# A packed product over 48 contraction rows, made a product over all 128 rows with zero weights below

## The chip, the cores and the metric

The kernel runs on one core of a Trainium2 chip. The metric is the device time in microseconds (us) of one execution; for one core that is the time of that core. A core has the engines TensorE (PE in the profile, its weight loads listed apart as PEld), VectorE (DVE), ScalarE (ACT), GpSimd (POOL) and SyncE (SP), which run their own instruction streams and wait for each other through semaphores, and 16 DMA engines that move data between HBM and the on-chip memory SBUF.

## What is computed

Cut to what matters, the reference is this:

```python
# x: (10000, 128), adj: (10000, 10000), float32
h = item_feat @ W_item.T + b_item              # (10000, 128)
b = layernorm(x) @ W_user.T + b_user
x = x + relu(adj @ h + b)                      # the big product
# then a mixture of 8 experts, top 1, with a capacity of 1563 rows each
n = layernorm(x); probs = softmax(n @ gate_w + gate_b); idx = argmax(probs)
x = x + y_of_expert[idx](n) * prob             # relu(n @ w1 + b1) @ w2 + b2
```

Nearly all of the arithmetic and all of the 400 MB that are read are `adj @ h`.

## The kernel before

**The big product.** The 10000 users (rows of `adj`) are taken in 20 blocks of 500. The host has transposed `adj`, so that a block is a stack of chunks of 128 items by 500 users: 78 full chunks (`FULL`) and a remainder of 16 items (`REM`). For each chunk TensorE holds 128 items x 128 features of `h` as weights and streams 500 users past them; the sums stay in one PSUM bank (`acc[q]`, two banks that blocks use in turn). Chunks are loaded in groups of 4, 20 groups a block (`GROUPS`), the last one of 2 full chunks and the remainder.

**Three products for one.** Matmuls run on operands of the reduced type fp32r, and the precision of fp32 is made up by splitting both sides into a high and a low part: `h_hi*a_hi` and `h_lo*a_hi` (`high_part`, L949 and L951) and `h_hi*a_lo` (`low_part`, L960). ScalarE makes `a_hi` from the loaded `raw` (`high`, L440), into a ring of 4 groups; VectorE subtracts and makes `a_lo` in place of `raw` (`low`, L604), a ring of 10 groups.

**The remainder.** The 16 items of the remainder are handled in one matmul, in place of three: `PACK` is 48, and the rows 0 to 47 of the last chunk of `h_hi` hold `h_hi`, `h_lo` and `h_hi` again, 16 rows each, against `a_hi`, `a_hi` and `a_lo` in the same rows of a slot of the ring. The rows 16 to 47 of the weights are put there once by two small DMAs (`pack_h`, issued on SP's queue in block 1). This is L967, once a block, 20 times in all. It ends the accumulation of its block (`stop=True`), and its end raises `lo_used`.

**Order on TensorE.** It is written out by hand, in `body`: `high_part` of group g, then `low_part` of group g-1, and small products for other stages after chosen groups. So the last `low_part` of a block, with L967 as its last matmul, stands behind `high_part` of group 0 of the next block and ahead of `high_part` of group 1. Behind the last block it stands by itself, ahead of the small products of that block's routing.

**Who waits for L967.** ScalarE waits for `lo_used` of the whole block before it casts group 3 of the next block (the ring slot of group 3 is the one that L967 reads), and before it takes the sums out of the bank (`take_gnn`, L449). SP waits for `lo_used` group by group before it reloads `raw`.

**Around it.** The blocks' routing (layernorm, gate, slots) runs on VectorE and GpSimd one and two blocks late, between the large instructions. GpSimd scatters each block's rows by indirect DMA (`scatter`, L849 and L853), 8 of them a block; in the last block it also clears unused slots (L860, L867, L875). After the 20 blocks comes the expert stage: 32 units of 392 rows, whose records are loaded by SP, with L1067 to L1098 on TensorE.

**Start.** VectorE fills some constants and raises `set_up` with each; TensorE waits for four of these (`pe.wait_ge(set_up, 4)`), for the constants and for the first items before its first product `h_chunks` (L932).

Of the kernel before, what the change touches and what calls it, by code (L numbers as in the profile page):

```python
# [5 lines left out]
ALU = mybir.AluOpType  # L6
# [6 lines left out]
HID = 128  # L13
# [6 lines left out]
BLOCK = TILES * TP  # L20
BLOCKS = USERS // BLOCK
FULL = ITEMS // 128
REM = ITEMS - FULL * 128
PACK = 3 * REM
CHUNKS = FULL + 1
# [5 lines left out]
HI_RING = 4  # L31
# [43 lines left out]
def build(nc, adj_m, adj_r, items_t, x, consts, item_consts, w1, w2, rec_d, out):  # L75
    ctx = ExitStack()
    with ctx:
        def sb(name, shape, dt=F32):
            return ctx.enter_context(nc.sbuf_tensor(name, shape, dt))

        def sem(name):
            return ctx.enter_context(nc.semaphore(name))
# [4 lines left out]
        def const(name, rows=128):  # L87
            a, b = COLS[name]
            return cst[0:rows, a:b]

        ident = const("ident")
        h_hi = sb("h_hi", [128, CHUNKS * HID], F32R)
# [6 lines left out]
        a_hi = sb("a_hi", [128, HI_RING, GMAX * BLOCK], F32R)  # L99
# [84 lines left out]
        acc = bank[0:2]  # L184
# [17 lines left out]
        set_up = sem("set_up")  # L202
# [75 lines left out]
        def blocks(eng, body):  # L278

            for i in range(PEEL // 2):  # L280
                for q in range(2):
                    body(i, q)
            with eng.Fori(PEEL // 2, BLOCKS // 2 - 1) as i:
                for q in range(2):
                    body(i, q)
            for q in range(2):
                body(BLOCKS // 2 - 1, q)
# [42 lines left out]
        @block.sync  # L330
        def _(sp):
            def load_items(g):
                if g >= 2:
                    sp.wait_ge(h_product, g - 1)
                a = FIRST[g] * 128
                b = min(a + SIZES[g] * 128, ITEMS)
                sp.dma_start(items[:, g % 2, 0:b - a], items_t[:, a:b]).then_inc(items_loaded[g % 2], 16)

            def body(i, q):
                b = i * 2 + q  # L340
                fixed = isinstance(b, int)
                for g in range(GROUPS):
                    if not fixed or b > 0 or g >= RAW:
                        sp.wait_ge(lo_used, b * GROUPS + g - RAW + 1)
                    last = g == GROUPS - 1
                    n = (SIZES[g] - last) * BLOCK
                    a = FIRST[g] * BLOCK
                    adj_b = adj_m[b] if fixed else adj_m[bass.ds(b, 1), :, :].rearrange("o p n -> (o p) n")
                    sp.dma_start(raw[:, g % RAW, 0:n], adj_b[:, a:a + n],
                                 max_dma_last_dim=16384).then_inc(raw_loaded[g % RAW], 16)  # L350
                    if fixed and b == 1 and g == 2:
                        pack_h()
                    if last:
                        rem_b = adj_r[b] if fixed else adj_r[bass.ds(b, 1), :, :].rearrange("o p n -> (o p) n")
                        sp.dma_start(raw[0:PACK, g % RAW, n:n + BLOCK], rem_b).then_inc(raw_loaded[g % RAW], 16)
                    if fixed and b == 0 and g + 2 < GROUPS:
                        load_items(g + 2)

            def pack_h():

                sp.wait_ge(h_lo_ready, GROUPS)
                cols = slice(FULL * HID, CHUNKS * HID)
                sp.dma_start(h_hi[REM:2 * REM, cols].bitcast(F32), h_lo[0:REM, cols].bitcast(F32)).then_inc(h_packed, 16)
                sp.dma_start(h_hi[2 * REM:PACK, cols].bitcast(F32), h_hi[0:REM, cols].bitcast(F32)).then_inc(h_packed, 16)

            sp.dma_start(cst[:, :], consts).then_inc(consts_loaded, 16)
            sp.dma_start(gnn[:, 0:2 * HID], item_consts).then_inc(consts_loaded, 16)
            load_items(0)
            load_items(1)
            blocks(sp, body)  # L370


            def load_weights(e, slot_, wait):
                if wait:
                    sp.wait_ge(yT_ready, (e - 1) * UNITS_E)
                w1_e = w1[bass.ds(e, 1), :, :].rearrange("o p n -> (o p) n")
                w2_e = w2[bass.ds(e, 1), :, :].rearrange("o p n -> (o p) n")
                sp.dma_start(wb1[:, slot_, :], w1_e).then_inc(weights_loaded[slot_], 16)
                sp.dma_start(wb2[:, slot_, :], w2_e).then_inc(weights_loaded[slot_], 16)

            rec_units = rec_d.rearrange("(r j) c -> r (j c)", j=4)

            def load_rec(q, k, wait):
                if wait:
                    sp.wait_ge(toki_ready, q - BODY + 1)
                    sp.wait_ge(yout_ready, q - BODY + 1)
                sp.dma_start(recq[:, k, :, :].rearrange("p j c -> p (j c)"),
                             rec_units[bass.ds(q * SLOT_P, SLOT_P), :]).then_inc(recq_loaded[k], 16)

            sp.wait_ge(edges_cleared, 16)  # L390
            sp.wait_ge(runs_cleared, EXPERTS * 16)
            sp.wait_ge(lo_used, BLOCKS * GROUPS)
            load_weights(0, 0, False)
            for q in range(2):
                sp.wait_ge(scattered[q], BLOCKS // 2 * TILES * 16)
            for k in range(BODY):
                if k == 2:
                    load_weights(1, 1, False)
                load_rec(k, k, False)
            with sp.Fori(1, UNITS // BODY) as i:  # L400
                for k in range(BODY):
                    if k % UNITS_E == 2:
                        load_weights(i * 2 + k // UNITS_E, k // UNITS_E, True)
                    load_rec(i * BODY + k, k, True)
            for q in range(2):
                sp.wait_ge(passed_on[q], BLOCKS // 2 * TILES * 16)
            for k in range(2):
                sp.wait_ge(sent[k], UNITS // 2 * 64)
# [157 lines left out]
        def _(dve):  # L566
            v = nc.vector
# [10 lines left out]
            def h_bias(g):  # L578
                dve.wait_ge(h_product, g + 1)
                n, a = SIZES[g], FIRST[g] * HID  # L580
                m = n - 1 if g == GROUPS - 1 else n
                last = v.tensor_tensor(h_raw[:, a:a + m * HID].rearrange("p (c d) -> p c d", d=HID),
                                       ps_h[g % 2][:, 0:m * HID].rearrange("p (c d) -> p c d", d=HID),
                                       b_item.unsqueeze(1).broadcast_to([128, m, HID]), ALU.add)
                if m < n:
                    last = v.tensor_tensor(h_raw[0:REM, a + m * HID:a + n * HID], ps_h[g % 2][0:REM, m * HID:n * HID],
                                           b_item[0:REM, :], ALU.add)
                last.then_inc(h_biased, 1)
# [178 lines left out]
            v.memset(neghalf[:, :], -0.5).then_inc(set_up, 1)  # L767
            dve.wait_ge(consts_loaded, 32)
            v.tensor_copy(tok[:, :, :].rearrange("p a j -> p (a j)"), const("tok", TP)).then_inc(set_up, 1)
            dve.wait_ge(set_up, 4)  # L770
            h_bias(0)
            h_low(0)
            h_bias(1)
# [56 lines left out]
        def _(pool):  # L830
# [60 lines left out]
                if not fixed or b < BLOCKS - 1:  # L891
                    x_scale(b + 1)

            pool.wait_ge(set_up, 4)
            x_scale(0)
            blocks(pool, body)
            x1_scale(BLOCKS - 1, 1)
# [26 lines left out]
        def _(pe):  # L924
# [30 lines left out]
            def low_part(b, q, g):  # L955

                pe.wait_ge(lo_ready, b * GROUPS + g + 1)
                for c in range(min(SIZES[g], FULL - FIRST[g])):
                    k = FIRST[g] + c
                    last = nc.tensor.matmul(acc[q][:, 0:BLOCK], h_hi[:, k * HID:(k + 1) * HID],  # L960
                                            a_lo[:, g % RAW, c * BLOCK:(c + 1) * BLOCK],
                                            start=False, stop=False)
                if g == GROUPS - 1:
                    if isinstance(b, int) and b == 0:
                        pe.wait_ge(h_packed, 32)
                    c = FULL - FIRST[g]
                    last = nc.tensor.matmul(acc[q][:, 0:BLOCK], h_hi[0:PACK, FULL * HID:CHUNKS * HID],  # L967
                                            a_hi[0:PACK, g % HI_RING, c * BLOCK:(c + 1) * BLOCK],
                                            start=False, stop=True)
                last.then_inc(lo_used, 1)  # L970

# [74 lines left out]
                        logits(b - 1)  # L1046

            pe.wait_ge(consts_loaded, 32)
            pe.wait_ge(set_up, 4)
            h_chunks(0)  # L1050
            h_chunks(1)
            blocks(pe, body)
            low_part(BLOCKS - 1, 1, GROUPS - 1)
            count(BLOCKS - 2)
            turn_gnn(BLOCKS - 1)
# [109 lines left out]
```

## Time and profile before

| | |
|---|---|
| runs of the kernel before | 1458.34 us median of 3 (1447.47, 1458.34, 1459.8) |
| the profiled execution | 1444.59 us, its span 1442.6 us |
| mean granted TensorE clock | 0.971 |
| TensorE busy | 1356.5 us, 94% of the span |
| VectorE, ScalarE, GpSimd busy | 1169.6, 981.6, 569.6 us |
| HBM read, written | 422.79 MB, 23.50 MB |
| L967, the packed product | 20 times, 9.9 us busy in all |

Busy is the union of the instructions' spans. Matmuls overlap, so the sum of their durations is longer than the time they take: how fast TensorE goes is read from where one matmul starts and where the next one does. The profiled execution was quicker than each of the three timed runs.

### The profile page before, as it was taken

The numbers are of one execution on the slowest core, as the hardware profiler recorded it, in microseconds if no ns is written. First come the engines' busy times: TensorE is split into PE (matmuls) and PEld (weight loads), VectorE is DVE, ScalarE is ACT, GpSimd is POOL, SyncE is SP. The second block draws the span as 40 slices with busy tenths as digits, with TensorE's granted clock in tenths as the row PEclk, the third lists the DMA queues.
The fourth block names the chain that finished last, engine by engine and source line by source line (L and its number), as shares of the span: only waits on it lengthen the run. The fifth ranks groups of instructions, "written<-read, shape, count | busy, mean of one in ns | idle before, by whom it ended". The sixth has DMA issues, their size and how long they took to land. (4 is left out here: it accounts for less than half of the span.)

```text
span 1442.6 us, 20384 instructions
## 1 busy us (share of the span) xinstructions
PE 1356.5 (94%) x6278; PEld 1109.0 (77%) x6278; DVE 1169.6 (81%) x1714; ACT 981.6 (68%) x1010; POOL 569.6 (39%) x426
## 2 busy tenths in 40 slices
PE   7999999999999999999999999999999952998893
PEld 6888888888888888888888888888888842776662
DVE  7898988989889889888898898898988931677665
ACT  5677876777768767767677687677776713877661
POOL 0001235144053251350541523514405365576777
PEclk9999999999999999999999999999999975999997
DMA  8999999999999999999999999999999723122220
GB/s 326 358 393 407 399 381 348 371 357 357 365 356 358 372 354 354 374 352 362 361 365 356 362 359 358 360 358 367 360 359 369 285 87 91 51 85 73 66 59 3
DMA packets 89072, 435.59 MB, mean 302 GB/s; under 512 B 22558, under 2 KB 24774, under 8 KB 89032
## 3 DMA queue, kind: packets, MB, share of 16 engines
q1 hardware_dynamic: 68000, 417.72, 78.4%
q0 software_dynamic: 17952, 12.25, 3.2%
q10 hardware_dynamic: 3080, 5.12, 1.1%
q8 instruction: 21, 0.34, 0.1%
q14 instruction: 19, 0.16, 0.0%
HBM read 422.79 MB, written 23.50 MB: 309 GB/s over the span
## 5 line engine op out<-in xcount | busy, mean ns | idle before, releaser
L604 DVE TENSOR_TENSOR a_lo<-raw,a_hi 128x2000 fp32r<-128x2000 f32 (+1 forms) x400 | 862.2, 2188 | 127.6 <-ACT a_hi L440 124.1
L440 ACT CAST a_hi<-raw 128x2000 fp32r<-128x2000 f32 (+1 forms) x400 | 721.4, 1826 | 180.8 <-PE bank L951 111.6
L949 PE MATMUL bank<-a_hi,h_hi 128*128 128x500 f32 x1560 | 626.2, 401 | 0.9 <-ACT a_hi L440 0.8
L951 PE MATMUL bank<-a_hi,h_lo 128*128 128x500 f32 x1560 | 606.9, 389 | 0.0
L960 PE MATMUL bank<-a_lo,h_hi 128*128 128x500 f32 x1560 | 417.9, 388 | 0.0
L949 PEld LDWEIGHTS bank<-a_hi,h_hi 128*128 128x128 f32 x1560 | 293.6, 188 | 65.9 <-issue 10.6
L951 PEld LDWEIGHTS bank<-a_hi,h_lo 128*128 128x128 f32 x1560 | 294.5, 189 | 59.1 <-issue 4.4
L960 PEld LDWEIGHTS bank<-a_lo,h_hi 128*128 128x128 f32 x1560 | 293.3, 188 | 59.3
L841 POOL TENSOR_TENSOR late<-ve,neghalf 125x4 f32<-125x4 f32 x20 | 57.2, 2861 | 649.6 <-DVE ve L621 649.6
L849 POOL DMA_INDIRECT records<-late,slot x80 | 182.3, 2278 | 22.9 <-issue 22.6
L915 POOL DMA_INDIRECT out<-raw,toki x128 | 136.5, 1066 | 37.1 <-issue 36.8
L853 POOL DMA_INDIRECT out<-late,kept_out x80 | 116.3, 1454 | 24.4 <-issue 24.4
L1098 PE MATMUL bank<-raw 128*128 128x392 f32 x256 | 92.5, 504 | 5.8 <-issue 5.8
L553 ACT ACTIVATE raw<-bank,raw 128x392 f32<-128x392 f32 x128 | 66.5, 587 | 21.4 <-remote 16.0
L481 ACT COPY colsT<-bank 128x500 f32<-128x500 f32 x20 | 11.5, 577 | 99.3 <-PE bank L1000 83.7
L1098 PEld LDWEIGHTS bank<-raw 128*128 128x128 f32 x256 | 49.3, 195 | 35.3 <-issue 9.3
L544 ACT ACTIVATE raw<-raw 98x128 f32<-98x128 f32 x128 | 53.1, 494 | 19.5 <-DMA raw<-records 19.5
L837 POOL TENSOR_TENSOR xrs<-xve,neghalf 125x4 f32<-125x4 f32 x20 | 26.5, 1327 | 89.5 <-DVE xve L621 89.1
L798 DVE TENSOR_TENSOR a_hi<-bank,a_hi 128x392 fp32r<-128x392 f32 x32 | 18.1, 564 | 51.8 <-ACT a_hi L538 41.2
L1087 PE MATMUL bank<-a_hi 128*128 128x392 f32 x128 | 48.5, 379 | 5.2 <-issue 2.9
L325 POOL TENSOR_TENSOR carrier_pool<-ones 125x1 f32<-125x1 f32 x52 | 34.0, 655 | 44.4 <-issue 36.1
L1089 PE MATMUL bank<-a_hi 128*128 128x392 f32 x128 | 45.5, 355 | 0.0
(116 smaller groups left out, 938.0 us busy)
## 6 DMA issues: line engine op xcount, KB each, us to landing
raw<-adj_m SPq DMA_DIRECT2D x380, 1000.0 KB, 6.7
raw<-adj_m SPq DMA_DIRECT2D x20, 500.0 KB
raw<-records SPq DMA_DIRECT2D x32, 202.1 KB
late<-items_t SPq DMA_DIRECT2D x19, 256.0 KB, 4.8
xb<-x ACTq DMA_DIRECT2D x20, 224.0 KB
raw<-w SPq DMA_DIRECT2D x8, 258.5 KB
raw<-w SPq DMA_DIRECT2D x8, 256.0 KB
out<-raw,toki POOLq DMA_INDIRECT x128
```

Of the source, the lines that this page charges most:

```text
L440: last = nc.scalar.copy(a_hi[:, g % HI_RING, 0:m], raw[:, g % RAW, 0:m])
L544: last = nc.scalar.activation(x2q[:, k % 2, j, :], recq[:, k, j, 0:HID], ACT.Identity, scale=recq[:, k, j, C_RSTD:C_RSTD + 1], bias=recq[: ...
L553: nc.scalar.activation(hm[:, (k - LAG_MID) % 2, f, :], ps_mid[f][:, 0:UNIT], ACT.Relu, bias=bias_of(k, LAG_MID, f)).then_inc(hm_ready, 1)
L604: last = v.tensor_tensor(a_lo[:, g % RAW, 0:m], raw[:, g % RAW, 0:m], a_hi[:, g % HI_RING, 0:m].bitcast(F32), ALU.subtract)
L841: p.tensor_tensor(rec[:, q, :, C_RSTD:C_RSTD + 1], ve[:, :].unsqueeze(2), neghalf[:, :].unsqueeze(2), ALU.pow).then_inc(rstd_ready, 1)
L849: p.indirect_dma_start(rec_d, bass.IndirectOffsetOnAxis(ap=slot[:, q, j:j + 1], axis=0), rec[:, q, j, :], None, bounds_check=SLOTS - 1, oo ...
L853: p.indirect_dma_start(out, bass.IndirectOffsetOnAxis(ap=kept_out[:, q, j:j + 1], axis=0), rec[:, q, j, 0:HID], None, bounds_check=USERS - ...
L915: p.indirect_dma_start(out, bass.IndirectOffsetOnAxis(ap=toki[:, (k - LAG_OUT) % BODY, j:j + 1], axis=0), yout[:, (k - LAG_OUT) % 2, j, :] ...
L949: nc.tensor.matmul(acc[q][:, 0:BLOCK], h_hi[:, k * HID:(k + 1) * HID], a, start=(k == 0), stop=False)
L951: last = nc.tensor.matmul(acc[q][:, 0:BLOCK], h_lo[:, k * HID:(k + 1) * HID], a, start=False, stop=False)
L960: last = nc.tensor.matmul(acc[q][:, 0:BLOCK], h_hi[:, k * HID:(k + 1) * HID], a_lo[:, g % RAW, c * BLOCK:(c + 1) * BLOCK], start=False, st ...
L1098: last = nc.tensor.matmul(ps_y[:, 0:UNIT], wb2[:, w, f * HID:(f + 1) * HID], hm[:, (k - LAG_Y) % 2, f, :], start=(f == 0), stop=(f == FC - 1))
```

## The change

L967 reads all 128 rows of the last chunk of `h_hi` and of the ring slot, in place of rows 0 to 47. So that rows 48 to 127 add nothing, VectorE writes zeros into rows 32 to 127 of the last chunk of `h_hi` at the start (two `tensor_scalar`, `ident` times 0.0, of 32 and of 64 rows by 128 columns), and `pack_h` fills rows 32 to 47 with `h_hi` later, now after a wait for the zeros. The ring slot's rows 48 to 127 hold there what an earlier group's cast left; it is multiplied by zero. `set_up` now counts to 6, and VectorE, GpSimd and TensorE wait for 6 in place of 4.

```diff
             def pack_h():
+                sp.wait_ge(set_up, 6)
                 sp.wait_ge(h_lo_ready, GROUPS)
...
             v.tensor_copy(tok[:, :, :].rearrange("p a j -> p (a j)"), const("tok", TP)).then_inc(set_up, 1)
-            dve.wait_ge(set_up, 4)
+            for lo, hi in ((32, 64), (64, 128)):
+                v.tensor_scalar(h_hi[lo:hi, FULL * HID:CHUNKS * HID], ident[lo:hi, :], 0.0, None,
+                                ALU.mult).then_inc(set_up, 1)
+            dve.wait_ge(set_up, 6)
             h_bias(0)
...
-            pool.wait_ge(set_up, 4)
+            pool.wait_ge(set_up, 6)
             x_scale(0)
...
-                    last = nc.tensor.matmul(acc[q][:, 0:BLOCK], h_hi[0:PACK, FULL * HID:CHUNKS * HID],
-                                            a_hi[0:PACK, g % HI_RING, c * BLOCK:(c + 1) * BLOCK],
+                    last = nc.tensor.matmul(acc[q][:, 0:BLOCK], h_hi[:, FULL * HID:CHUNKS * HID],
+                                            a_hi[:, g % HI_RING, c * BLOCK:(c + 1) * BLOCK],
                                             start=False, stop=True)
...
-            pe.wait_ge(set_up, 4)
+            pe.wait_ge(set_up, 6)
             h_chunks(0)
```

No instruction changes places on TensorE, ScalarE, GpSimd or SP. On VectorE two rows are added at its start. Before:

```order
L767 MEMSET neghalf 125x4
L769 COPY tok<-cst 125x8
L582 TENSOR_TENSOR h_raw_49<-bank5,gnn 128x512
L594 TENSOR_TENSOR h_lo<-h_raw_49,h_hi 128x512
L582 TENSOR_TENSOR h_raw_49<-bank6,gnn 128x512
```

And in the changed kernel:

```order
L768 MEMSET neghalf 125x4
L770 COPY tok<-cst 125x8
L772 TENSOR_SCALAR h_hi<-cst 32x128
L772 TENSOR_SCALAR h_hi<-cst 64x128
L583 TENSOR_TENSOR h_raw_49<-bank5,gnn 128x512
L595 TENSOR_TENSOR h_lo<-h_raw_49,h_hi 128x512
L583 TENSOR_TENSOR h_raw_49<-bank6,gnn 128x512
```

The two zero writes stand between the last of the old constants and the first bias of `h`, and TensorE's first product waits for them.

## Rows read from the trace of the kernel before

**Rows 1.** The page: granted TensorE clock in 40 slices of the span.

```profile
PEclk9999999999999999999999999999999975999997
```

**Rows 2.** Busy time by stage: blocks 2 to 18, and all that follows block 19's big product.

```profile
core 0: us, PE busy (x) PEld busy (x) DVE busy (x) ACT busy (x) POOL busy (x), PEclk, DMA share, GB/s
143.00:1112.00 969.00, 969.00 (x4432) 797.58 (x4431) 842.76 (x1155) 695.07 (x561) 350.06 (x187) 1.00 0.99 363
1170.30:1442.60 272.30, 194.49 (x921) 150.64 (x920) 156.35 (x355) 152.05 (x336) 180.75 (x220) 0.85 0.24 67
```

**Rows 3.** Line L967 from 143 to 1112 us: its matmuls (ns), and who waited.

```profile
L967 PE MATMUL bank<-a_hi,h_hi x17: 494/494/494, 143.4 to 1057.0; 48*128 48x500 f32 x17
...
  ACT a_hi L440: 39.0, 17
```

**Rows 4.** Timeline of PE, 598 to 603 us: start, us, engine, line, instruction.

```profile
599.45 0.39 PE L951 MATMUL bank<-a_hi,h_lo 128*128 128x500 f32 x1
599.68 0.61 PE L960 MATMUL bank<-a_lo,h_hi 128*128 128x500 f32 x2
600.22 0.49 PE L967 MATMUL bank<-a_hi,h_hi 48*128 48x500 f32 x1
600.64 0.49 PE L949 MATMUL bank<-a_hi,h_hi 128*128 128x500 f32 x1
600.98 0.39 PE L951 MATMUL bank<-a_hi,h_lo 128*128 128x500 f32 x1
...
602.57 0.62 PE L960 MATMUL bank<-a_lo,h_hi 128*128 128x500 f32 x2
```

**Rows 5.** Timeline of the weight loads there; in brackets the idle time ahead.

```profile
600.22 0.18 PEld L967 LDWEIGHTS bank<-a_hi,h_hi 48*128 48x128 f32 x1 [0.34 <-issue]
600.64 0.19 PEld L949 LDWEIGHTS bank<-a_hi,h_hi 128*128 128x128 f32 x1 [0.24 <-issue]
```

**Rows 6.** Timeline of PE, 610 to 612.5 us: the matmul behind L1013 and L1014.

```profile
611.98 0.47 PE L949 MATMUL bank<-a_hi,h_hi 128*128 128x500 f32 x1
```

**Rows 7.** Waits from 143 to 1112 us: total, times, longest.

```profile
DVE a_lo L604 <- ACT a_hi L440: 114.3, 51, 5.8
ACT a_hi L440 <- PE bank L951: 105.5, 128, 1.7
```

**Rows 8.** Timelines of the start, and of VectorE at 82 us.

```profile
5.67 0.17 DVE L769 COPY tok<-cst 125x8 f32<-125x8 f32 x1 [4.64 <-DMA gnn<-item_consts]
6.29 3.49 PEld L932 LDWEIGHTS bank<-gnn,late 128*128 128x128 f32 x16 [6.29 <-DMA gnn<-item_consts]
...
82.20 0.27 DVE L596 TENSOR_TENSOR h_lo<-h_raw,h_hi 16x128 fp32r<-16x128 f32 x1
```

**Rows 9.** Timelines of ScalarE, VectorE and GpSimd in the last block and behind it.

```profile
1114.73 3.63 ACT L440 CAST a_hi<-raw 128x2000 fp32r<-128x2000 f32 x2 [2.33 <-PE bank L967]
...
1116.62 2.24 DVE L604 TENSOR_TENSOR a_lo<-raw,a_hi 128x2000 fp32r<-128x2000 f32 x1 [0.48 <-ACT a_hi L440]
...
1149.52 8.69 DVE L604 TENSOR_TENSOR a_lo<-raw,a_hi 128x2000 fp32r<-128x2000 f32 x4
...
1175.21 0.17 DVE L621 TENSOR_SCALAR ve<-mv 125x4 f32<-125x4 f32 x1
...
1141.09 2.94 POOL L841 TENSOR_TENSOR late<-ve,neghalf 125x4 f32<-125x4 f32 x1 [33.22 <-DVE ve L621]
...
1149.79 9.48 POOL L849 DMA_INDIRECT records<-late,slot  x1 [0.30 <-DVE clear_edge L701]
...
1161.48 1.19 POOL L849 DMA_INDIRECT records<-late,slot  x1 [0.30 <-issue]
...
1182.08 1.05 POOL L841 TENSOR_TENSOR late<-ve,neghalf 125x4 f32<-125x4 f32 x1
```

**Rows 10.** The chain that ended last, in the expert stage.

```profile
1303.84 4.50 PE bank L1098 x8
...
1316.84 2.64 PE bank L1098 x8
```

## The prediction

> **What bounds the kernel now.** I read the stages first. [...] A busy TensorE is not yet a TensorE at its pace, so next I look at the pace. L967 starts 17 times between 143.4 and 1057.0 us [rows 3]: 913.6 us over 16 blocks is 57.10 us a block. [...]
>
> [...]
>
> **What one packed product costs.** I read distances from start to start. Between L951 at 600.98 and the L960 pair at 602.57 lie seven ordinary distances, 1.59 us, so 0.227 us for one matmul of 500 columns [rows 4]. From the L960 pair at 599.68 over L967 at 600.22 and L949 at 600.64 to L951 at 600.98 lie four distances: at the ordinary pace 0.91 us, in the trace 1.30. So a packed product costs 0.39 us more than an ordinary one in its place. The parts: the second L960 starts one ordinary distance behind 599.68, at 599.91, so L967 follows it by 0.31 (0.08 too much); L949 follows L967 by 0.42 (0.19 too much); L951 follows L949 by 0.34 (0.11 too much). The weight loads show the shape of it. Ordinarily a weight load runs beside the matmul ahead of it; here the load of L967 starts together with its matmul, after 0.34 us in which the load path did nothing ("issue": no event that the profile knows), and the next load, of L949, again starts with its matmul after 0.24 us [rows 5]. The stall stands on both sides of the one instruction whose rows are 48. L967 itself lasts 0.494 us in place of some 0.39, the same in all 17 [rows 3, 4].
>
> What is different about L967? Its type, its 500 columns and its 128 weight columns are those of its neighbours. Its sum closes a bank and the next matmul writes the other bank, but each block boundary changes banks between groups, and the step from L951 of the new block to L960 of the old one (599.45 to 599.68) is ordinary [rows 4]. It raises a semaphore, but so does the last L960 of every group. What is left is the number of rows, 48 against 128. By that reading, the change makes it an ordinary matmul.
>
> [...]
>
> **The change, part by part.**
> - *The stall goes*, 0.39 us for each packed product with ordinary matmuls on both sides. Twenty products; for the last one only L967's late start and its longer duration could count, 0.08 + 0.11 = 0.19.
> - *The path to the end* takes fewer than all of them. In the last block the cast of group 3 begins when L967 of block 18 is done (ScalarE had waited 2.33 us for it), VectorE's L604 at 1116.62 waited for that cast, and from there VectorE runs without a pause up to the variance that releases GpSimd's L841 at 1141.09 [rows 9]. GpSimd then works without a pause through scatters and clears until 1182.08, where it takes up a variance that VectorE had finished at 1175.38. So the end hangs on GpSimd, which hangs on the end of L967 of block 18. What TensorE wins after that (0.30 behind this L967, 0.19 at the last) runs into GpSimd's lead of 1182.08 - 1175.38 = 6.70 us and is worth nothing. On the path lie 18 whole stalls, of blocks 0 to 17, and 0.19 of block 18: 18 x 0.39 + 0.19 = 7.2 us. If all of TensorE's gain counted it would be 19 x 0.39 + 0.19 = 7.6.
> - *What is late next in a block*: the cast of group 3 waits for L967's end. ScalarE waits 39.0 us in 17 times for it, 2.3 each, and then needs 1.8 us. TensorE wants group 3 four parts behind L967, after `high_part` 1, `low_part` 0, `high_part` 2 and `low_part` 1: 24 matmuls of 0.227, or 5.4 us. The slack is 3.5 us against the 0.30 that L967's end comes closer, so this stays covered. The loads move 363 GB/s and must go 0.7% faster; the waits show no lateness there [rows 7].
> - *Two zero writes at the start.* The trace has no such instruction. The nearest rows are the copy ahead of it, 0.17 us, and a subtraction of 128 columns, 0.27 [rows 8]. The copy ends at 5.84, so the zeros are done between 6.18 and 6.38; TensorE's first weight load began at 6.29, put down to a DMA. The cost is 0 to 0.1 us, and it would go on to all that follows since the first products release the item loads. Nothing can get earlier by it. I take 0.05.
> - *The other waits*: SP's new wait in `pack_h` stands ahead of a wait for the last part of `h_lo`, made at 82.20 us [rows 8], long after the zeros; the reloads of `raw` queued behind are not held up by it. GpSimd's first work needs a variance that VectorE makes behind the first two biases of `h`, after the zeros in any case. Both cost nothing.
> - *More rows read*: weight load 0.18 against 0.19 for the neighbours [rows 5], so at most 0.01 a block, and beside other work.
>
> Sum: 7.2 - 0.05 = about 7.1 us. The profiled execution took 1444.59 us (2.0 of it outside the span of 1442.6), which gives 1437.5. That execution was the quickest of the four known; the median of the timed runs is 1458.34, and against that the same saving gives **1451.2 us**, a ratio of 0.995. The spread of the runs before, 1447.47 to 1459.8, is larger than the effect. Within 1% is about what a measurement of this kernel can tell from no change.
>
> **Rivals.**
> 1. *The stall has another cause and stays.* For it: the 0.47 us duration of an L949 behind the small products of 125 rows [rows 6] is much like the 0.49 behind L967, so a long L949 alone needs no 48 rows (the small products have another type, which L967 has not). Against it: the idle load path ahead of L967 itself. Time: 1458.3, or 1444.6 for the profiled one. [...] Chance 0.10.
> 2. *A scatter of the last block falls under VectorE.* The scatter at 1149.79 took 9.48 us against 1.19 at 1161.48; VectorE ran four L604 in a row beside it, 8.69 us from 1149.52 [rows 9]. That is a price of 8.3 us on the path that sets the end. GpSimd and VectorE hang on the same L967, so their distance should stay; if it moves by the few tenths that let one more scatter begin inside such a run, 8.3 is lost and 7.1 won: **1.2 us slower than before**, 1459.5. It decides from the point at which a scatter that now ends in time begins inside such a run. The same mechanism the other way would free up to the 6.70 us of lead, and give 1444.5. [...] Chance 0.04 slower, 0.04 faster.
> 3. *The expert stage meets more of the low clock.* [...] Chance 0.04 for four or more.
>
> **How the numbers follow.** The forecast has 0.78, and the four cases above 0.22. Its own range runs from 1437.0 (the quickest execution less 7.6) to 1452.7 (the slowest less 7.1). To hold the time 8 times in 10 I take 1435 to 1456, a stretch of low clock less at one end and two more at the other; most of rival 1 is left out. Faster by over 1% needs 14.6 us: the freed scatter, or runs of the two kernels that fall at different ends of a spread of 12.3; 0.12. Slower by over 1% needs the reverse without the gain: 0.03. Within 1%: 0.85.
>
> **What the profile of the changed kernel would show.** L967's successor with 128 rows, some 0.39 us long, its weight load beside the matmul ahead of it and with no idle time of 0.34; the next L949 0.227 behind it. L967's successor starts every 56.7 us in place of 57.10. TensorE still fully busy from 143 us on. ScalarE still waits at group 3, about as long as now. First weight load at 6.3 to 6.4. The last packed product near 1162.4, GpSimd's second L841 near 1175. Wrong would be: a distance that stays at 0.42 behind it; a block that is shorter while the span is not, which would put the loss into GpSimd's scatters or the expert stage.

## The result, and the profile of the changed kernel

| | before | changed |
|---|---|---|
| median of 22 runs | 1455.03 us (1441.31 to 1464.82) | 1446.91 us (1435.42 to 1454.16) |
| ratio of the times | | 0.9955, 95% interval 0.9936 to 0.9974 |
| profiled execution, its span | 1444.59, 1442.6 us | 1449.17, 1447.2 us |

The change makes the kernel 0.45% faster by the ratio, 6.5 us of 1455 (the two medians lie 8.1 us apart). The two profiled executions alone would say the opposite, by 4.6 us, so the profile must be read stage by stage. First the timeline of TensorE at the packed product (now L971) of the changed kernel:

```profile
596.55 0.61 PE L964 MATMUL bank<-a_lo,h_hi 128*128 128x500 f32 x2
597.00 0.39 PE L971 MATMUL bank<-a_hi,h_hi 128*128 128x500 f32 x1
597.23 0.39 PE L953 MATMUL bank<-a_hi,h_hi 128*128 128x500 f32 x1
597.45 0.39 PE L955 MATMUL bank<-a_hi,h_lo 128*128 128x500 f32 x1
```

and of its weight loads:

```profile
596.32 0.42 PEld L964 LDWEIGHTS bank<-a_lo,h_hi 128*128 128x128 f32 x2
596.78 0.19 PEld L971 LDWEIGHTS bank<-a_hi,h_hi 128*128 128x128 f32 x1
597.00 0.19 PEld L953 LDWEIGHTS bank<-a_hi,h_hi 128*128 128x128 f32 x1
```

The four distances that took 1.30 us in [rows 4] take 0.90 here. The load of L971 starts 0.22 us ahead of its matmul, beside the matmul before it, and neither load has an idle time in brackets, where [rows 5] have 0.34 and 0.24. The line's own view, from 138 to 1104 us, and the busy times of the stages:

```profile
L971 PE MATMUL bank<-a_hi,h_hi x17: 392/392/392, 143.3 to 1050.7; 128*128 128x500 f32 x17
...
  ACT a_hi L441: 35.8, 17
```

```profile
core 0: us, PE busy (x) PEld busy (x) DVE busy (x) ACT busy (x) POOL busy (x), PEclk, DMA share, GB/s
143.00:1105.00 962.00, 962.00 (x4430) 798.64 (x4428) 842.21 (x1155) 693.99 (x561) 346.70 (x187) 1.00 0.99 365
1162.80:1447.20 284.40, 200.12 (x922) 150.16 (x920) 156.47 (x355) 153.22 (x336) 177.60 (x221) 0.85 0.23 64
```

907.4 us over 16 blocks is 56.71 us a block, against 57.10 in [rows 3]: 0.39 less, with TensorE still busy all the time. The stage behind the big product took 284.40 us against 272.30 in [rows 2], 12.1 longer; that is the whole of the contradiction. The change has no instruction there. On the quicker chips of the experiments the stage is as long with the stall as without it: from the start of the last packed product to the end of the span it took 257.9 us with 48 rows (all of the change but the matmul, below) and 257.6 in the changed kernel, one trace each.

The timeline of GpSimd in the last block and behind it, and that of the start, VectorE and TensorE:

```profile
1134.28 2.93 POOL L845 TENSOR_TENSOR late<-ve,neghalf 125x4 f32<-125x4 f32 x1 [33.02 <-DVE ve L622]
...
1142.96 9.49 POOL L853 DMA_INDIRECT records<-late,slot  x1 [0.30 <-DVE clear_edge L702]
...
1175.08 1.06 POOL L845 TENSOR_TENSOR late<-ve,neghalf 125x4 f32<-125x4 f32 x1
1182.73 0.20 POOL L325 TENSOR_TENSOR carrier_pool<-ones 125x1 f32<-125x1 f32 x1 [6.60 <-issue]
```

```profile
5.37 0.17 DVE L770 COPY tok<-cst 125x8 f32<-125x8 f32 x1 [4.34 <-DMA gnn<-item_consts]
5.57 0.47 DVE L772 TENSOR_SCALAR h_hi<-cst 32x128 fp32r<-32x128 f32 x2
...
6.14 3.58 PE L936 MATMUL bank<-gnn,late 128*128 128x128 f32 x16 [6.14 <-DVE h_hi L772]
```

GpSimd's second L845 starts at 1175.08 in place of 1182.08 [rows 9], 7.0 us earlier, with the same long scatter ahead of it (9.49 against 9.48). The zeros end at 6.04 and TensorE's first product starts at 6.14, released by them. In the kernel before a load of items released it:

```profile
6.32 0.98 PE L932 MATMUL bank<-gnn,late 128*128 128x128 f32 x3 [6.32 <-DMA late<-items_t]
```

From the start of VectorE's copy of the constants to the first product it is 0.65 us there (5.67 in [rows 8] to 6.32), and 0.77 in the changed kernel.

### The profile page after: what moved, and what is told of

The parts are those of the page before. It is cut to its first block and busy times, and to the rows that moved or that the text cites. A ratio compares the mean times of both kernels' runs of the same rounds, so it can differ in the third digit from the quotient of the medians.

```text
span 1447.2 us, 20387 instructions
## 1 busy us (share of the span) xinstructions
PE 1354.0 (94%) x6278; PEld 1110.0 (77%) x6278; DVE 1169.5 (81%) x1716; ACT 981.9 (68%) x1010; POOL 562.4 (39%) x426
## 3 DMA queue, kind: packets, MB, share of 16 engines
q1 hardware_dynamic: 68000, 417.72, 77.8%
## 5 line engine op out<-in xcount | busy, mean ns | idle before, releaser
L845 POOL TENSOR_TENSOR late<-ve,neghalf 125x4 f32<-125x4 f32 x20 | 57.2, 2859 | 645.8 <-DVE ve L622 645.8
L853 POOL DMA_INDIRECT records<-late,slot x80 | 178.7, 2233 | 22.9 <-issue 22.6
L919 POOL DMA_INDIRECT out<-raw,toki x128 | 132.6, 1036 | 38.6 <-issue 38.3
L1102 PE MATMUL bank<-raw 128*128 128x392 f32 x256 | 96.9, 523 | 9.2 <-issue 6.9
```

The source lines that it names most:

```text
L845: p.tensor_tensor(rec[:, q, :, C_RSTD:C_RSTD + 1], ve[:, :].unsqueeze(2), neghalf[:, :].unsqueeze(2), ALU.pow).then_inc(rstd_ready, 1)
L853: p.indirect_dma_start(rec_d, bass.IndirectOffsetOnAxis(ap=slot[:, q, j:j + 1], axis=0), rec[:, q, j, :], None, bounds_check=SLOTS - 1, oo ...
L919: p.indirect_dma_start(out, bass.IndirectOffsetOnAxis(ap=toki[:, (k - LAG_OUT) % BODY, j:j + 1], axis=0), yout[:, (k - LAG_OUT) % 2, j, :] ...
L1102: last = nc.tensor.matmul(ps_y[:, 0:UNIT], wb2[:, w, f * HID:(f + 1) * HID], hm[:, (k - LAG_Y) % 2, f, :], start=(f == 0), stop=(f == FC - 1))
```

## The experiments

They ran on three chips, each beside runs of the kernel before: 64 rows, 96 rows, all but the matmul and two in a row beside a single one of 1429.06 us; 32 rows, the padding, the early clears and the changed kernel again beside a median of 1429.37 (9 runs); the two with pauses beside a median of 1429.04 (7 runs). Only the changed kernel again, the early clears, and the clears with the pauses were timed more than once; the others are single executions, and are read by their traces. All these runs of the kernel before are quicker than every one of the 22 above, and lie closer together.

### How many rows stall: 64, 96, 32

```diff
-                    last = nc.tensor.matmul(acc[q][:, 0:BLOCK], h_hi[:, FULL * HID:CHUNKS * HID],
-                                            a_hi[:, g % HI_RING, c * BLOCK:(c + 1) * BLOCK],
+                    last = nc.tensor.matmul(acc[q][:, 0:BLOCK], h_hi[0:64, FULL * HID:CHUNKS * HID],
+                                            a_hi[0:64, g % HI_RING, c * BLOCK:(c + 1) * BLOCK],
                                             start=False, stop=True)
```

(and 0:96, 0:32 in the same places of the changed kernel).

> The changed kernel with the packed product over rows 0 to 63 in place of all 128. If a matmul over at most 64 rows among full ones is what stalls TensorE, the stall is whole again: the product starts 0.31 us behind its predecessor and its successor 0.42 behind it, 57.10 us a block. If the stall hung on the odd count of 48 or on a partly filled group of 32 rows (48 is one and a half), 64 rows are free of it: 0.227 on both sides, 56.71 us a block.

> The changed kernel with the packed product over rows 0 to 95. If only products of at most 64 rows change how the array is divided, this one is ordinary: 0.227 us on both sides, 56.71 us a block. If any row count other than that of the neighbours stalls, 0.31 and 0.42 are back and a block takes 57.10 us.

> The changed kernel with the packed product over rows 0 to 31 (the low part of the adjacency's remainder is left out). If a change of the division costs the same whichever it is, 0.31 and 0.42 us, 57.10 us a block, as with 48 and 64 rows. If the stall follows the number of rows, it differs from that of 48.

The view of line L971 from 143 to 1080 us in the kernel with 64 rows:

```profile
L971 PE MATMUL bank<-a_hi,h_hi x17: 494/494/494, 142.9 to 1056.5; 64*128 64x500 f32 x17
```

with 96 rows:

```profile
L971 PE MATMUL bank<-a_hi,h_hi x16: 391/391/392, 199.1 to 1049.7; 96*128 96x500 f32 x16
```

with 32 rows:

```profile
L971 PE MATMUL bank<-a_hi,h_hi x17: 492/492/493, 143.0 to 1056.5; 32*128 32x500 f32 x17
```

64 rows: 913.6 over 16 is 57.10 us a block, the stall is whole, 1427.51 us in all. 32 rows: 913.5 over 16 is 57.09, 1431.6 us. 96 rows: 850.6 over 15 (the first product of the other views falls just ahead of 143 us here) is 56.71, no stall, 1420.4 us. So it is no matter of rows that fill a group of 32, nor of being equal to the neighbours: 32, 48 and 64 rows cost the same, 96 and 128 cost nothing. The limit lies above 64 and not above 96; no run had a number in between. What TensorE does inside at the change is not shown: the "division" that the expectations here and below speak of was my reading, and no run places products of 32 and of 64 rows next to each other. The weight loads of the kernel with 64 rows show the picture of [rows 5] again:

```profile
599.72 0.18 PEld L971 LDWEIGHTS bank<-a_hi,h_hi 64*128 64x128 f32 x1 [0.34 <-issue]
600.14 0.19 PEld L953 LDWEIGHTS bank<-a_hi,h_hi 128*128 128x128 f32 x1 [0.24 <-issue]
```

### All of the change but the matmul

```diff
-                    last = nc.tensor.matmul(acc[q][:, 0:BLOCK], h_hi[:, FULL * HID:CHUNKS * HID],
-                                            a_hi[:, g % HI_RING, c * BLOCK:(c + 1) * BLOCK],
+                    last = nc.tensor.matmul(acc[q][:, 0:BLOCK], h_hi[0:48, FULL * HID:CHUNKS * HID],
+                                            a_hi[0:48, g % HI_RING, c * BLOCK:(c + 1) * BLOCK],
                                             start=False, stop=True)
```

> The changed kernel with everything of the change but the matmul itself: the zero writes and the waits for six stay, the product reads rows 0 to 47. By my theory the whole gain is in the rows of the matmul: 57.10 us a block as before, stall 0.31 and 0.42, and a start that is as in the changed kernel. If the zeros or the waits did something, the block is shorter than 57.10.

```profile
L971 PE MATMUL bank<-a_hi,h_hi x17: 494/494/494, 143.2 to 1056.8; 48*128 48x500 f32 x17
```

That is the view of L971 there: 57.10 us a block, 1429.41 us against 1429.06. The zeros and the waits for them neither give nor cost anything that one run can tell; the gain is in the rows of the matmul.

### Two packed products in a row

```diff
+                    nc.tensor.matmul(acc[q][:, 0:BLOCK], h_hi[0:PACK, FULL * HID:CHUNKS * HID],
+                                     a_hi[0:PACK, g % HI_RING, c * BLOCK:(c + 1) * BLOCK],
+                                     start=False, stop=False)
                     last = nc.tensor.matmul(acc[q][:, 0:BLOCK], h_hi[0:PACK, FULL * HID:CHUNKS * HID],
```

> The kernel before with its packed product of 48 rows issued twice in a row (the remainder of 16 items is added twice; this changes the result). If the stall is paid for each change of division, the second one costs an ordinary 0.23 us and a block takes 57.10 + 0.23 = 57.33 us. If it is paid for each such instruction (its weights never load beside another matmul), the second starts some 0.42 us behind the first, or more, and a block takes 57.5 us or more.

TensorE's timeline, where L967 is the added product and L970 the old one:

```profile
601.06 0.61 PE L960 MATMUL bank<-a_lo,h_hi 128*128 128x500 f32 x2
601.60 0.49 PE L967 MATMUL bank<-a_hi,h_hi 48*128 48x500 f32 x1
601.93 0.38 PE L970 MATMUL bank<-a_hi,h_hi 48*128 48x500 f32 x1
602.24 0.49 PE L949 MATMUL bank<-a_hi,h_hi 128*128 128x500 f32 x1
602.58 0.38 PE L951 MATMUL bank<-a_hi,h_lo 128*128 128x500 f32 x1
```

and the loads:

```profile
601.60 0.18 PEld L967 LDWEIGHTS bank<-a_hi,h_hi 48*128 48x128 f32 x1 [0.34 <-issue]
601.71 0.19 PEld L970 LDWEIGHTS bank<-a_hi,h_hi 48*128 48x128 f32 x1
602.24 0.19 PEld L949 LDWEIGHTS bank<-a_hi,h_hi 128*128 128x128 f32 x1 [0.35 <-issue]
```

Five distances take 1.52 us, 0.39 more than five ordinary ones (1.13): the same excess as for one packed product. L967 starts from 143.1 to 1060.1 us, 17 times, so a block takes 57.31 us, 0.21 more than with one. The load of the second packed product goes beside the first; only the loads at the two changes stand alone. So the price is paid for the pair of changes, from a full product to one of 48 rows and back, and not for each product. The 0.42 behind a lone packed product [rows 4] splits here into 0.33 and 0.31, each some 0.1 over the ordinary 0.227: part of it belongs to the way in (the matmul behind the first changed one is late too), part to the way out.

### Is TensorE's end the end that counts?

```diff
+                    if isinstance(b, int) and b == BLOCKS - 1:
+                        for _ in range(20):
+                            nc.tensor.matmul(acc[q][:, 0:BLOCK], h_hi[:, FULL * HID:CHUNKS * HID],
+                                             a_hi[:, g % HI_RING, c * BLOCK:(c + 1) * BLOCK],
+                                             start=False, stop=False)
```

> The changed kernel with 20 more ordinary packed products in front of the last one of block 19 (they add the remainder again in that block, which changes its result). That is 20 x 0.227 = 4.5 us more on TensorE at the end of the big product. If GpSimd's chain sets the start of the last stage, its lead of 6.7 us swallows it: the second L845 stays near 1175.1 us and its wait for VectorE stays away, and what TensorE had won behind block 18 would indeed be worth nothing. If TensorE's end sets it, it moves by 4.5 us to 1179.6.

TensorE's and GpSimd's timelines:

```profile
1162.28 4.72 PE L973 MATMUL bank<-a_hi,h_hi 128*128 128x500 f32 x20
1166.84 0.39 PE L976 MATMUL bank<-a_hi,h_hi 128*128 128x500 f32 x1
...
1174.59 1.06 POOL L845 TENSOR_TENSOR late<-ve,neghalf 125x4 f32<-125x4 f32 x1
```

4.56 us more on TensorE moved nothing on GpSimd: L845 at 1174.59 (1174.77 without the padding on the same chip), 1421.26 us against a median of 1421.92. So what TensorE won behind L967 of block 18, well under a microsecond, is worth nothing, as step two of the sum had it.

### The changed kernel again, and the clears taken off GpSimd's chain

```diff
                 fixed = isinstance(b, int)
+                if fixed and b == BLOCKS - 1:
+                    set_zeros()
+                    clear_slots()
                 if not fixed or b > 0:
                     x1_scale(b - 1, 1 - q)
                 if not fixed or b > 1:
                     scatter(b - 2, q)
                 if fixed and b == BLOCKS - 1:
-                    set_zeros()
                     clear_edges()
-                    clear_slots()
...
-                    if g == 12 and fixed and b == BLOCKS - 1:
+                    if g == 8 and fixed and b == BLOCKS - 1:
                         find_unused()
```

> The changed kernel itself, timed beside the version with early clears on one chip. Forecast: 0.995 of the kernel before, with an interval of about 0.004 on either side, since the expert stage moves both by several microseconds from run to run. A block takes 56.71 us.

> The changed kernel with GpSimd's clearing of unused runs (memset and 8 indirect DMAs) moved in the last block ahead of its work on blocks 18 and 17, where it waits, and VectorE's instructions for it at group 8 in place of 12. In the changed kernel GpSimd works without a pause from 1134 to 1175.08 us and takes up then a variance that VectorE had at 1168.40. If that chain sets the end, up to 6.7 us come off: the second L845 near 1168.5 and the time 0.4 to 0.5% below the changed kernel, near 0.991 of the kernel before. If the scatters of block 17 are pushed later under VectorE's four long subtractions, most of it is lost, within 2 us of the changed kernel. Theory two, that the end of the big product on TensorE sets the start of the last stage, gives no gain at all.

On the same chip the changed kernel took 1421.92 us (1421.02 to 1422.24, 5 runs), ratio 0.9946 (0.9932 to 0.9959); the early clears 1412.94 us (1412.13 to 1414.41, 4 runs), ratio 0.9888 (0.9873 to 0.9903). They gave 9.0 us where 6.7 was the bound that I had put. GpSimd's timeline, first of the changed kernel on this chip:

```profile
1133.99 2.93 POOL L845 TENSOR_TENSOR late<-ve,neghalf 125x4 f32<-125x4 f32 x1 [33.02 <-DVE ve L622]
...
1174.77 1.05 POOL L845 TENSOR_TENSOR late<-ve,neghalf 125x4 f32<-125x4 f32 x1
1182.80 0.20 POOL L325 TENSOR_TENSOR carrier_pool<-ones 125x1 f32<-125x1 f32 x1 [6.98 <-issue]
1183.69 1.28 POOL L853 DMA_INDIRECT records<-late,slot  x1 [0.69 <-issue]
```

then with the clears early:

```profile
1148.27 10.61 POOL L853 DMA_INDIRECT records<-late,slot  x1 [0.30 <-DVE clear_edge L702]
...
1172.00 1.04 POOL L845 TENSOR_TENSOR late<-ve,neghalf 125x4 f32<-125x4 f32 x1 [2.88 <-DVE ve L622]
1173.78 0.20 POOL L325 TENSOR_TENSOR carrier_pool<-ones 125x1 f32<-125x1 f32 x1 [0.73 <-DVE slot L728]
1174.68 1.26 POOL L853 DMA_INDIRECT records<-late,slot  x1 [0.71 <-issue]
```

L845 came only 2.8 us earlier, but the scatter of block 18 came 9.0 earlier. Between the two stood an idle time of 6.98 us "issue". Ahead of that scatter the program waits for the clears to have landed; with the clears over 30 us earlier, the wait is 0.73 and ended by VectorE. The view of the clears (tile `clear_runs`) in the changed kernel on this chip has their landing:

```profile
L879 POOL DMA_INDIRECT records<-h_raw,clear_runs x8: 931/935/955, 1165.1 to 1173.8; - x8
DMA to landing us min/median/max: 3.8/4.4/8.9
```

The last clear is issued at 1173.8. If the longest landing is its own, it has landed at 1182.7, just ahead of GpSimd's next instruction at 1182.80; with the padding the same sum is 1173.64 + 8.3 = 1181.9, and GpSimd goes on at 1182.03. So the second L845, which I took for the end of the chain, had slack behind it: by these sums the last clear's transfer was later. Both hang on the same GpSimd chain and so moved by the same 7 us in the change (the scatter of block 18 from 1190.73 to 1183.63), which is why the sum did not suffer.

### The long scatter

```diff
+        spare = sb("spare", [1, 36])
...
                     low(b, g)
+                    if fixed and b == BLOCKS - 1 and 15 <= g <= 17:
+                        for n in range(12):
+                            v.memset(spare[:, (g - 15) * 12 + n:(g - 15) * 12 + n + 1], 0.0)
```

> The changed kernel with 12 one-element memsets on VectorE behind each of its subtractions for groups 15, 16 and 17 of block 19, where it ran four in a row (8.69 us) while one of GpSimd's scatters took 9.49 us. If VectorE's large subtractions of two SBUF operands keep GpSimd out while they run back to back, the pauses of roughly 0.8 us let the scatter go on: it takes some 3 us, the following ones are no longer than 3, and GpSimd's second L845 comes 2 to 6 us earlier than 1174.8. If the scatter was long for another reason (its descriptors, the records' transfer), it stays at 9 us and everything behind it where it was.

> Both: the clears early and the memsets between the subtractions of block 19. The early clears gave 0.989 of the kernel before; there VectorE's L644 waited for the block's scatters until 1169.69 us, where its input from TensorE was there from about 1164. If the pauses shorten the 10.6 us scatter to some 3 us, L644 starts near 1165 and up to 4.5 us more come off: about 0.986. If not, 0.989 again.

GpSimd's timeline with the pauses alone:

```profile
1132.66 2.93 POOL L849 TENSOR_TENSOR late<-ve,neghalf 125x4 f32<-125x4 f32 x1 [33.04 <-DVE ve L623]
...
1141.35 3.04 POOL L857 DMA_INDIRECT records<-late,slot  x1 [0.30 <-DVE clear_edge L703]
1144.69 2.00 POOL L857 DMA_INDIRECT records<-late,slot  x1 [0.31 <-issue]
...
1169.58 1.06 POOL L849 TENSOR_TENSOR late<-ve,neghalf 125x4 f32<-125x4 f32 x1
```

The scatter took 3.04 us in place of 9.49, and the second L849 (the renumbered L845) came 5.2 us earlier than 1174.77; the single time was 1416.13 us. Not all of the 5.2 is the pauses' doing: this execution was 1.3 us ahead from the first packed product on (85.4 against 86.7 us), and the first L849, ahead of the pauses, was 1.3 earlier too (1132.66 against 1133.99). From the first to the second it took 36.9 us in place of 40.8, so the pauses gave 3.9. The scatter alone became 6.45 shorter; the next three took 2.0 us each, where they had taken 1.41, 1.20 and 1.19. The pauses were far smaller than the 0.8 us that I expected. VectorE's timeline has

```profile
1143.39 2.24 DVE L606 TENSOR_TENSOR a_lo<-raw,a_hi 128x2000 fp32r<-128x2000 f32 x1
1143.40 2.37 DVE L739 MEMSET spare<- 1x1 f32 x13
1145.71 2.24 DVE L606 TENSOR_TENSOR a_lo<-raw,a_hi 128x2000 fp32r<-128x2000 f32 x1
```

so the subtractions start 2.32 us apart, against 2.15 where four of 2.24 filled 8.69 us. Some 0.17 us more between the starts of two subtractions was enough here for a scatter of 3.04 us in place of 9.49, and the scatters behind it then started 2.3 us apart, as the subtractions did. With early clears too it is 1409.46 us (1407.87 to 1410.5, 4 runs), ratio 0.9856 (0.984 to 0.9873): the quickest version of all, and L645 (the renumbered L644) starts at 1165.29 in place of 1169.69. GpSimd begins the scatter of block 18 at 1170.28 in place of 1174.68, 4.4 us earlier, with clears that start at the same time in both (1127.0). That a scatter is long beside subtractions that run back to back and short beside spaced ones is measured (9.49 us against 3.04); what held it is not shown.

## Why the prediction was right, point by point

- **What bounds it.** TensorE at its full pace, from 143 us to the last block: right. It stayed fully busy (962.00 of 962.00 us from 143 to 1105, at a granted clock of 1.00, as in [rows 2]; VectorE had 842.21 there, ScalarE 693.99), and each block lost what the stream lost, 0.39 us.
- **The price of one packed product**, 0.39 us: right (57.10 to 56.71), and shown to be the rows of this matmul, by undoing them alone (57.10 again) and by going to 96 (56.71).
- **The path to the end**, 18 stalls and 0.19, 7.2 us: right. The second L845 came 7.0 us earlier; the time on one chip fell by 1429.37 - 1421.92 = 7.5 us, and over the 22 runs by 6.5, both within the interval. The step behind it was incomplete: I named GpSimd's next instruction as the end, and the landing of its clears was what was late. That both move together was not worked out beforehand, so this part of the sum was right with some luck. The lead that I put at 6.70 us was larger for the same reason: in the changed kernel VectorE's slots for block 18 were done at 1170.08, and GpSimd went on at 1182.73.
- **The zeros**, 0 to 0.1 us: not shown to be within the bound. They now release TensorE's first product, 0.10 us after they end. From the copy of the constants to that product it takes 0.77 us, against 0.65 in the kernel before and 0.56 in it with two packed products, where a load released it: up to 0.12 or 0.21 us for the zeros, if the loads were there in time. The first weight load came at 6.11 and not at 6.3 to 6.4, since the constants landed 0.3 earlier in this execution. Against a saving of 7 us either is nothing.
- **What is late next**: nothing was. ScalarE waits 35.8 us in 17 times at group 3, where [rows 3] have 39.0, and the load rate rose from 363 to 365 GB/s.
- **The absolute time.** 1451.2 was forecast and 1446.91 measured. The ratio was right to 0.0005 (0.995 against 0.9955); most of the rest is that three runs stood for the kernel before, whose median over 22 is 1455.03. The ends of the range count one stretch of low clock less and two more: no run shows that number, it was my estimate. What the trace shows is the price of one, 1.86 us: eight L1098 took 4.50 us at 1303.84 [rows 10], at a granted clock of 0.63, and 2.64 us at 1316.84, at 1.00.
- **Rival 1** (another cause) fell with the runs of 48, 64 and 96 rows. A lone product among full ones lasts 0.492 us with 32 rows against 0.392 with 128, and costs 0.38 us more a block (57.09 against 56.71); the second of two packed products in a row lasts 0.38 us. The L949 of 0.47 us behind small products [rows 6] was not looked into.
- **Rival 2** (a scatter under VectorE's run) did not come: 9.49 against 9.48 us, since both engines hang on the same matmul. That a scatter is longer beside subtractions without a pause is borne out (9.49 against 3.04 us), but the price was too high: I put 8.3 us on the path, and taking it away shortened the scatter by 6.45 and the path to the second L849 by 3.9. And the freed scatter would not have reached "faster by over 1%", for which I named it: 7.1 + 6.70 = 13.8 us, short of 14.6.
- **Rival 3** (the expert stage) is what the pair of profiled executions seems to show: 12.1 us longer with the change. The experiments speak against the change as the cause: from the last packed product to the end of the span, 256.3 to 260.4 us in the four executions with the stall (32, 48 and 64 rows, two in a row), 256.5 and 257.6 in two without (96 and 128 rows). The mean granted clock of the stage is 0.85 in both of the pair and in the changed kernel's 257.50 (1162.5 to 1420 us); TensorE's busy time (194.49, 200.12, 189.26 us) and its idle time (77.8, 84.3, 68.2) both differ. What makes the stage some 15 and 27 us longer in the profiled pair stays open.

## What to carry to other kernels

Among full matmuls of this kind (fp32r, 500 columns), one over 64 rows or fewer (32, 48 and 64 were measured) costs 0.38 to 0.39 us more a block than one over all 128: fill the rows with zeros, or put the small ones in a row, since the price was for the change and back (a second one of 48 rows behind the first added 0.21 us a block, no more than an ordinary matmul's 0.227). Where the bounding engine has no idle time at all, look for lost time in the distances from start to start: this stall shows in no wait of a compute engine and in no share of TensorE's busy time, only in the idle time ahead of two weight loads (0.34 and 0.24 us). And ask at the end of the dense stage whose chain the next stage hangs on; here two small edits of that chain (clears earlier, 0.17 us pauses) took the ratio to the kernel before from 0.9946 to 0.9856, some 12.5 us, more than the change itself.

## What the runs showed of the hardware that was not expected

- The extra cost of 32, 48 and 64 rows is the same to 0.01 us a block (57.09, 57.10, 57.10), and at 96 rows it is gone (56.71).
- An indirect DMA's issue on GpSimd took 10.61 us beside five large VectorE subtractions that ran back to back, and another 9.49 beside four, but 3.04 when these stood 2.32 us apart in place of 2.15.
- GpSimd went on 6.98 us after its second L845 had ended (the changed kernel timed again): eight indirect DMAs of 112 rows took 3.8 to 8.9 us from issue to landing, half of them up to 4.4. If the longest landing is that of the last one, it ended at 1182.7, and GpSimd's next instruction started at 1182.80.
